# Three phases of a routed-attention block: separate loops with keys folded into queries, and one schedule of slots with queries, keys and row-tiled scores

## What is computed

```python
# x: 16 batches of 256 rows of 128
mod = (silu(c) @ wmod)                                  # shifts, scales and gates, per batch
h = layernorm(x) * (1 + ca) + sa
x = x + ga * causal_attention(h, W, b)                  # "first attention": one head, 256 x 256
h = layernorm(x) * (1 + cb) + sb
# light: windows of 128 rows, 8 heads of 64
xn = rmsnorm(h, gamma_light)
light = softmax(q @ k.T * 64**-0.5) @ v @ wo_light      # q, k, v = xn @ wq, xn @ wkv, per window and head
# selection: 50 iterations of a soft top-k on 2 scores per row, then the top 128 rows
def body(_, ab):
    a = logk - logsumexp(s + b)
    b = -relu(s + a)
scores = exp(s + a + b); sel, idx = top_k(scores, n)
# heavy: 128 selected rows attend to all 256 rows of their batch, 8 heads of 64
heavy = softmax(qh @ kh.T * 64**-0.5) @ (vh * scores_kv) @ wo_heavy
x = x + gb * (light + scatter(heavy * scores_q))
```

## Time and profile before

| | us |
|---|---|
| median of 3 runs | 541.76 (539.86 to 545.21) |
| the profiled execution | 540.5 |
| its span, first to last instruction | 538.7 |
| TensorE busy | 480.9 |
| ScalarE busy | 396.4 |
| VectorE busy | 387.7 |
| GpSimd busy | 259.9 |

### The profile page before, as it was taken

One profiled execution on the slowest core, in us unless ns is written; L12 is line 12 of the kernel. 1 busy time (PEld: TensorE's weight loads), 2 busy tenths in 40 slices (PEclk: granted clock), 3 DMA queues, 4 the chain that ended last, 5 costly groups with the idle time before them and its releaser, 6 DMA issues.

```text
span 538.7 us, 12047 instructions
## 1 busy us (share of the span) xinstructions
PE 480.9 (89%) x3805; PEld 414.2 (77%) x3805; DVE 387.7 (72%) x1311; ACT 396.4 (74%) x1480; POOL 259.9 (48%) x294
## 2 busy tenths in 40 slices
PE   2498878766999999999999798899999999999995
PEld 1386656545888888888888676798898988888984
DVE  5539999985888888888888798365656656556652
ACT  2269899856999999999999567666666676666662
POOL 6316577772334333334433123454556665556555
PEclk9999999978999999999999889999999999999998
DMA  8740101100000000000000000000000100000101
GB/s 233 258 204 2 31 21 31 31 30 19 2 12 12 12 11 11 12 11 12 11 12 12 12 10 12 21 19 8 12 12 11 16 16 12 12 12 11 16 7 16
DMA packets 18398, 16.42 MB, mean 30 GB/s; under 512 B 1984, under 2 KB 17104, under 8 KB 18080
## 3 DMA queue, kind: packets, MB, share of 16 engines
q1 hardware_dynamic: 14336, 11.83, 6.8%
q0 software_dynamic: 3248, 3.41, 3.7%
q10 hardware_dynamic: 752, 0.40, 0.3%
HBM read 10.36 MB, written 5.28 MB: 29 GB/s over the span
## 4 chain that ended last, share of the span: by engine, by line
PE 69%; DVE 7%; ACT 2%; issue 1%; POOL 1%; POOLq 0%; DVEq 0%
PE bank L651 13%; PE bank L653 10%; PE bank L652 10%; PE bank L884 6%; PE bank L932 6%; PE bank L834 6%; PE bank L916 5%; PE bank L852 5%; PE bank L819 4%; PE bank L949 2%; ACT pr L584 1%; DVE left L1250 1%; DVE top_at L1251 1%; DVE nmx L1218 1%; DVE top_all L1247 1%
## 5 line engine op out<-in xcount | busy, mean ns | idle before, releaser
L402 POOL TENSOR_TENSOR pr<-pr,rinv 128x512 f32<-128x512 f32 x64 | 66.7, 1042 | 134.8 <-DVE rinv L1224 134.7
L417 POOL TENSOR_TENSOR pr<-pr,rinv 128x512 f32<-128x512 f32 x64 | 72.5, 1133 | 76.6 <-DVE rinv L1327 76.4
L584 ACT ACTIVATE pr<-bank,nmx 128x128 f32<-128x128 f32 x256 | 89.7, 364 | 8.0 <-DVE nmx L1218 7.9
L628 ACT ACTIVATE pr<-bank,nmx 128x256 f32<-128x256 f32 x128 | 59.7, 472 | 34.0 <-DVE nmx L1321 33.9
L1218 DVE TENSOR_REDUCE nmx<-bank 128x4 f32<-128x512 f32 x64 | 43.5, 680 | 28.8 <-PE bank L653 27.2
L584 ACT ACTIVATION_READ_ACCUMULATOR pr<-bank,nmx 128x1 f32 x256 | 52.5, 205 | 0.0
L819 PE MATMUL bank<-ident,pr 128*128 128x128 f32 x256 | 39.6, 278 | 5.8 <-POOL pr L402 5.8
L1321 DVE TENSOR_REDUCE nmx<-bank 128x2 f32<-128x512 f32 x64 | 43.8, 684 | 0.7 <-PE bank L653 0.4
L884 PE MATMUL bank<-xq,T_w 128*128 128x128 f32 x256 | 41.8, 286 | 0.4 <-ACT xq L613 0.4
L638 ACT ACTIVATE pt<-bank 128x512 f32<-128x512 f32 x64 | 38.4, 600 | 1.4 <-PE bank L916 1.4
L916 PE MATMUL bank<-ident,pr 128*128 128x128 f32 x256 | 38.5, 273 | 0.4 <-POOL pr L417 0.4
(11 more groups left out here) (231 smaller groups left out, 1506.9 us busy)
## 6 DMA issues: line engine op xcount, KB each, us to landing
mod_bc<-mod_rows_scratch SPq DMA_DIRECT2D x1, 3072.0 KB, 11.1
X<-in_L_attn_x SPq DMA_DIRECT2D x4, 512.0 KB, 10.3
xh_scratch<-xhs SPq DMA_DIRECT2D x16, 128.0 KB, 1.8
out<-X SPq DMA_DIRECT2D x16, 128.0 KB, 1.8
mod_bc<-mod_rows_scratch SPq DMA_DIRECT2D x1, 1024.0 KB, 4.2
wkv_raw<-in_L_ffn_wkv_light SPq DMA_DIRECT2D x1, 512.0 KB, 11.8
wmod_sb<-in_L_wmod ACTq DMA_DIRECT2D x1, 384.0 KB, 5.1
wq_raw<-in_L_ffn_wq_heavy POOLq DMA_DIRECT2D x1, 256.0 KB, 7.5
```

Of the source, the lines that this page charges most:

```text
L402: pool.tensor_tensor(q, q, rinv[k % 4][:, :, None].broadcast_to([P, 4, P]), ALU.mult)\
L417: pool.tensor_tensor(q, q, rinv[k % 4][:, 0:2, None].broadcast_to([P, 2, N]), ALU.mult)\
L584: act.activation(pr[k % 4][:, i * P:(i + 1) * P], ps[2 + k % 2][:, i * P:(i + 1) * P], ACT.Exp, bias=nmx[k % 4][:, i:i + 1], accum_out=sum ...
```

## The change

The three pipelines become one list of (phase, lag, function) for each engine, run in 158 slots. Batch b of first attention starts in slot 5b/2 rounded down, light unit g in slot 14 + g, heavy unit g in slot 78 + g; selection's steps have slots of their own between 49 and 76. `early` now holds only what the weights' preparation needs, and PSUM banks are given to uses by tables (`FILL_BANKS` before slot 14, `A_BANKS` after); P^T has one bank instead of two, light values and output share one.

Scores come from queries and keys: `Q_w`, `K_w` (split raw weights) instead of the product `U_w`; `QH_w` (f32), `KH_w` instead of `T_w`. The scores are f32 matmuls with 64 contraction rows, even heads in rows 0 to 63 and bank 2, odd heads in rows 64 to 127 and bank 3. Q and K are one f32 copy each, on ScalarE or VectorE in turn, and no low half.

An iteration of selection works on e = exp(s - c): u becomes the sum over min(e, u)/k, one VectorE instruction; the base c is renewed twice (`SEGMENTS`), with one exp and one ln each. `xhat` moves from VectorE to GpSimd. The two broadcasts of gamma (`gam_bc`) go.

```diff
+A_AT = [5 * b // 2 for b in range(B)]
+SCORES_AT = A_AT[-1] + 12
+H0 = SCORES_AT + 29
+L0 = H0 - 4 * B
+END = H0 + 4 * B + 16
+
+
+def run_slots(stages):
+
+    for t in range(END):
+        for phase, lag, f in stages:
+            if phase == "A":
+                if t - lag in A_AT:
+                    f(A_AT.index(t - lag))
+            elif phase == "L":
+                if 0 <= t - lag - L0 < 4 * B:
+                    f(t - lag - L0)
+            elif phase == "H":
+                if 0 <= t - lag - H0 < 4 * B:
+                    f(t - lag - H0)
+            else:
+                f(t)
...
+        SEGMENTS = (0, 17, 33, CD_ITERS - 1)
+        ITERATIONS_AT = {SCORES_AT + at: (n, n + count) for at, n, count in (
+            (3, 0, 6), (4, 6, 6), (5, 12, 5), (8, 17, 6), (9, 23, 6), (10, 29, 4), (13, 33, 6), (14, 39, 6), (15, 45, 4))}
+        LN_AT = [SCORES_AT + at for at in (6, 11, 16)]
+        TOP_AT = SCORES_AT + 18
...
+        A_LAGS = {"s": 4, "x": 13, "h": 2, "qk": 3, "o": 7, "p": 5, "v": 4}
+        A_BANKS = {"x": 5, "h": 5, "s": 1, "o": 1, "p": 5, "qk": 1, "v": 5}
+        FILL_BANKS = {"x": 6, "h": 5, "s": 2, "o": 3, "p": 4, "qk": 1, "v": 5}
...
-                    mm = triple(ps[7 * (j == 1)][:, i * N:(i + 1) * N], [u[:, 2 * j + i, :] for u in U_w],
+                    c = 2 * (j % 2) + i
+                    mm = triple(ps[7 * (j == 1)][:, i * N:(i + 1) * N], [w[:, c * P:(c + 1) * P] for w in (Q_w, K_w)[j // 2]],
                                 (XT_hi[:, b, :], XT_lo[:, b, :]))
-                mm.then_inc(lt["up"], 1)
-
...
-            def scores(p, k):
...
-                at_least(pe, lt["p"], 4 * (g - 1))
-                triple(ps[2 + k % 2][:, :].rearrange("p (h t) -> p h t", h=4),
-                       [t[:, b, w * P:(w + 1) * P] for t in (XT_hi, XT_lo)],
...
+            def scores(g):
...
+                at_least(pe, lt["p"], 8 * window)
+                for c in range(4):
+                    for i in range(2):
+                        rows = slice(i * DH, (i + 1) * DH)
+                        mm = pe.matmul(ps[2 + i][:, c * P:(c + 1) * P], QT[b % 2][rows, c, t], KT[b % 2][rows, c, t],
+                                       start=True, stop=True)
...
-            def scores_h(p, k):
...
-                for i in range(2):
-                    mm = triple(ps[2 + k % 2][:, i * N:(i + 1) * N], [u[:, 2 * j + i, 0:NQ] for u in U[par]],
-                                (XT_hi[:, b, :], XT_lo[:, b, :]))
...
+            def scores_h(g):
...
+                for m in range(2):
+                    for i in range(2):
+                        rows, c = slice(i * DH, (i + 1) * DH), 2 * n + m
+                        mm = pe.matmul(ps[2 + i][:, m * N:(m + 1) * N], QT[b % 2][rows, c, 0:NQ], KT[b % 2][rows, c, :],
+                                       start=True, stop=True)
                 mm.then_inc(hv["Sp"], 1)
...
+                for c in range(4):
+                    mm = pe.matmul(ps[0][:, c * NQ:(c + 1) * NQ], QH_w[:, c * P:(c + 1) * P], xq[b % 2][:, :],
+                                   start=True, stop=True)
...
+            def project_kh(g):
...
                 for i in range(2):
-                    mm = pe.matmul(ps[0][:, i * NQ:(i + 1) * NQ], T_w[:, 2 * j + i, :], xq[par][:, :],
-                                   start=True, stop=True)
-                mm.then_inc(hv["tp"], 1)
...
-            run_phases(([(0, h_transpose), (2, value_a), (3, values_a), (1, scores_a), (0, query_key),
-                             (2, p_transpose_a), (6, x_transpose)], extra_a),
-                       ([(3, scores), (0, project), (OUT_LAG, out_light), (5, p_transpose), (0, project_v), (6, values)],
-                        selection),
-                       ([(6, values_h), (0, row_transpose), (0, project_vh), (4, p_transpose_h),
-                         (0, project_h), (9, out_heavy), (1, scores_h)], None),
-                       "al al al al la la la", "lh lh lh lh lh lh lh")
+            run_slots([("A", 4, scores_a), ("A", 13, x_transpose), ("L", 7, p_transpose), ("A", 2, h_transpose),
+                       ("L", 0, project), ("A", 3, query_key), ("A", 7, values_a), ("L", 1, project_v),
+                       ("A", 5, p_transpose_a), ("H", 0, row_transpose), ("A", 4, value_a), ("H", 1, project_kh),
+                       ("H", 8, p_transpose_h), ("H", 0, project_q), ("H", 3, project_vh), ("H", 10, values_h),
+                       ("L", 9, values), ("H", 4, scores_h), ("T", 0, heavy_piece), ("H", 12, out_heavy),
+                       ("L", 10, out_light), ("T", 0, selection), ("L", 4, scores)])
...
+            def split(w, source, gamma, n):
+                dve.tensor_scalar(w[0][:, :], source, gamma, None, ALU.mult).then_inc(w_hi, 1)
+                dve.wait_ge(w_hi, n + 1)
+                dve.scalar_tensor_tensor(w[1][:, :], source, gamma, w[0][:, :].bitcast(F32), ALU.mult, ALU.subtract)\
+                    .then_inc(w_split, 1)
...
-            def cd_sums(n):
-                act.wait_ge(r["t"], n + 1)
-                at_least(act, r["ln"], n)
-                act.activation(cd_e[:, :], cd_t[:, :], ACT.Exp, accum_out=cd_sum[:, :]).then_inc(r["e"], 1)
-                act.wait_ge(r["e"], n + 1)
-                act.activation(cd_ln[:, :], cd_sum[:, :], ACT.Ln).then_inc(r["ln"], 1)
...
+            def cd_iteration(n):
+                if n in SEGMENTS:
+                    dve.wait_ge(r["e"], SEGMENTS.index(n) + 1)
+                    u = u_first
+                else:
+                    dve.wait_ge(r["u"], n)
+                    u = cd_u[(n - 1) % 2]
+                dve.scalar_tensor_tensor(cd_min[:, :], cd_e[:, :], u[:, :], inv_k[:, :], ALU.min, ALU.mult,
+                                         accum_out=cd_u[n % 2][:, :]).then_inc(r["u"], 1)
...
+            def cd_rebase(s):
+                dve.wait_ge(r["ln"], s + 1)
+                dve.tensor_scalar(cd_c[:, :], cd_ln[:, :], cd_c[:, :], 40.0, ALU.add, ALU.subtract).then_inc(r["c"], 1)
+                dve.wait_ge(r["c"], s + 2)
+                dve.tensor_scalar(cd_t[:, :], s_rows[:, :], cd_c[:, :], 70.0, ALU.subtract, ALU.min).then_inc(r["t"], 1)
...
+            run_slots([("L", 6, recip), ("T", 0, select_1), ("L", 5, neg_max_pair), ("A", 4, mask_max),
+                       ("A", 4, neg_max_a), ("L", 11, finish_light), ("A", 13, xt_lo), ("A", 9, neg_mean_rstd2),
+                       ("A", 8, ln2_stats), ("H", 11, o_evac_h), ("L", 7, pt_evac), ("L", 0, project_evac),
+                       ("A", 7, attn_out), ("A", 4, v_evac), ("T", 0, select_2), ("A", 12, keep_scores),
+                       ("H", 1, k_evac_h), ("H", 5, neg_max_pair_h), ("H", 6, recip_h), ("A", 8, aggregate),
+                       ("H", 13, finish_heavy), ("T", 0, select_3), ("T", 0, weights), ("A", 10, route),
+                       ("A", 10, norm_squares), ("H", 3, v_evac_h), ("A", 8, var_eps), ("T", 0, late_mean),
+                       ("A", 4, recip_a)])
...
+            run_slots([("L", 2, v_evac_l), ("A", 1, ln1), ("A", 13, xt_hi), ("L", 10, o_evac), ("H", 5, exps_odd_h),
+                       ("H", 8, pt_evac_h), ("H", 1, k_evac_h), ("T", 0, cd_act), ("A", 2, h_evac), ("L", 5, exps_odd),
+                       ("L", 7, pt_evac_act), ("L", 5, exps_even), ("H", 1, xq_evac), ("H", 5, exps_even_h),
+                       ("A", 3, qk_evac), ("L", 0, project_evac), ("A", 9, ln2), ("A", 5, pt_evac_a),
+                       ("H", 0, q_evac_h), ("A", 4, exps_a), ("A", 10, squares)])
...
+            run_slots([("A", 9, ln2_rstd), ("H", 14, scatter), ("A", 10, modulate), ("L", 6, normalise),
+                       ("T", 0, gather_first), ("A", 10, rms), ("A", 7, residual), ("L", 11, add_light),
+                       ("A", 11, xhat), ("H", 0, gather), ("H", 7, normalise_h)])
```

More of the change, by code:

```diff
@@ L199, in adaln_routed_attention @@
         nmxa = [sb(f"nmxa{i}", [P, C]) for i in two]
-        pa = [sb(f"pa{i}", [P, 3 * P]) for i in two]
         suma = [sb(f"suma{i}", [P, C]) for i in two]
@@ L218, in adaln_routed_attention @@
         s4 = [sb(f"s4{i}", [P, 4]) for i in two]
-        early.close()
-        sb = late
-        U = [[sb(f"U{i}{s}", [P, HEADS, N], F32R) for s in ("hi", "lo")] for i in two]
+        QT = [sb(f"QT{i}", [P, 4, N]) for i in two]
+        KT = [sb(f"KT{i}", [P, 4, N]) for i in two]
         V = [sb(f"V{i}", [P, C, HID]) for i in two]
-        pr = [sb(f"pr{i}", [P, 512]) for i in range(4)]
         nmx = [sb(f"nmx{i}", [P, 4]) for i in range(4)]
@@ L228, in adaln_routed_attention @@
         rinv = [sb(f"rinv{i}", [P, 4]) for i in range(4)]
+        tmp = [sb(f"tmp{i}", [P, D]) for i in two]
+        early = ExitStack()
+        late = sb
+        sb = lambda name, shape, dt=F32: early.enter_context(nc.sbuf_tensor(name, shape, dt))
+        wmod_sb = sb("wmod_sb", [P, 6 * D])
+        wq_raw = sb("wq_raw", [P, 2, HID])
+        wkv_raw = sb("wkv_raw", [P, 2 * HID])
+        wk_hT = sb("wk_hT", [P, 4, D])
```

(67 more changed lines are left out.)

1134 lines of the change are left out of this document (518 added, 616 removed).

## The result

| | before | after |
|---|---|---|
| median of the runs | 542.73 us (539.86 to 545.21) | 516.28 us (513.88 to 519.6) |
| ratio to before | | 0.952, 95% interval 0.944 to 0.960 |
| span of the profiled run | 538.7 us | 517.8 us |
| TensorE busy | 480.9 us, 89% | 461.0 us, 89% |

The account below looks back on a forecast made before the run. TensorE bounds most of the kernel (89% of span), ScalarE and VectorE first attention, VectorE selection's end. Start 47 + work 434 - 16 already done + tail 8 = 473; selection 8 and waits 12 give 493, plus 3: 496 us, range 472 to 528.

Parts of the forecast that it names:

- The likeliest case: Whole kernel: the sum of terms holds, 496 us, own range 478 to 510, chance 0.50.
- two rivals: ScalarE paces the overlapped slots, 518 us, chance 0.19; weight loads of the two halves don't overlap, 520, chance 0.14.
- Light scores: Light phase: 16 f32 instructions on alternating row halves take 1.03 us a window, bounds 1.78 and 2.32; batch 12.2 us.
- the rival of the other side: Light and heavy scores: halves of rows don't run together at all; 545 or 580 us, chance 0.12.
- Loads in turn: Scores: weight loads of the two halves don't overlap, light scores at 1.78 us; +24 us, 520, chance 0.14.
- Start: Before light work: VectorE begins slot 4 at about 25, ten slots of 1.90 us, slot 14 at 47 (44 to 50).
- Overlapped slots: First attention beside light work: TensorE leads at 4.61 us a slot, plus 0.3 of waits, 12 us over 36 slots.
- Selection: Selection's 9 + 8 slots: VectorE needs 3.9 to 4.7 us against TensorE's 3.05; 14 us at most, 8 taken.
- Heavy batch: Heavy phase on TensorE: 11.1 us a batch instead of 11.52, bounds 12.6 and 13.7; sixteen take 177 us.
- Light work's rest, heavy phase and end: From slot 76 on: the sum leaves 205.7 us, with heavy batches of 11.1 us and a tail of 8.
- No overlap in effect: First attention and light phase: light values first come at 138.81 as before, only the phases' gains remain; 521 us, chance 0.05.
- the marks given: Signs of being right: TensorE at least 93% of span, first QT projection before 55 us, light scores 1.0 to 1.1 us.

Follow-up runs that it names:

- the fastest kernel: Kernel after, with the selection iterations' exponentials in PSUM and light output in bank 5 from the 13th window on: 502.5 us, 0.929 of before.

## Why the prediction was right, and where it was not

Faster by over 1%, forecast at 0.88, and 516 lies in 472 to 528. The likeliest case said 496, 20 us too low, outside its own range of 478 to 510. It is the width of the range that holds the result: two rivals had 518 and 520, nearest to it, and neither of their mechanisms came about. By the terms of its sum, on the profiled span (517.8 against 493):

**Light scores: right.** 1.03 forecast, 1.09 measured; light batch 12.2 forecast, 12.33 measured where nothing disturbs it (the kernel without overlap, from 271 us on). The mechanism named for it, halves running together, is shown by the run without it: 566.0 us, between the 545 and 580 given to the rival of the other side. "Loads in turn" has fallen: the light block takes 1.09, not 1.78, with alternating halves., the one 64-row row of before, was no bad price for halves that don't alternate: 0.145 us an instruction, 0.124 in that run.

**Start: 4 us short, most of it scatter.** Slot 14 at 51.05 against 47; it came at 48.3 when the kernel ran again, and at 47.7 to 49.5 in the variants with the same code up to there. The sum let ten slots run at VectorE's 1.90 us.

**Overlapped slots: right.** From its own terms, first attention's remaining 46 us, 36 units of light work (110), 11 of waits, less what the lags leave over at slot 50 (some 14: three transposes, four values blocks, five outputs at rates of the earlier trace rows and two scores; this is an estimate made afterwards), 153 us; measured 51.05 to 203.18, 152.1. TensorE stands still for 8.6 us of it, where 11 were given. ScalarE did not pace them: it is busy 131.7 us of the 152.1, TensorE 143.5.

**Selection: the term that failed, 8 us forecast, 21 measured (19 when run again).** The load of VectorE was right in kind. The sum over it was not: "14 us at most" is what its slots of 3.9 us give (17 x 0.85). With its other price, 9 slots of 4.7 and 8 of 3.9, it is 9 x 1.65 + 8 x 0.85 = 22, so the forecast's own upper bound holds what was measured, and 8 was taken under a bound set too low. And two things were not in it. The iteration was priced by a top round, which reads one tensor; with two in SBUF it collides with GpSimd, on average 0.595 us and 0.07 for the sum instead of at most 0.55. And "banks are shared in turn: fits" looked at P^T alone: with values and output in one bank, VectorE's lateness stops TensorE at once. With both mended the excess is 6.5 us, near the 8 forecast. Nor was there a term for TensorE's clock, 0.95 in these slots: some 5 us of the 21.

**Heavy batch: 11.1 forecast, 11.38 measured, 16 x 0.28 = 4.5 us.** Scores 1.06 for 1.03 twice, K 1.64 for 1.60 and Q 0.99 for 0.89 make 0.20 of it. The earlier trace rows had priced only projections behind f32; Q behind transposes is dearer too. The other 0.08 is open.

**Light work's rest, heavy phase and end (slot 76 on): 8 us short in all**, 214.1 measured where the sum leaves 205.7, the 4.5 among them. Two more are the drain: TensorE waits twice 0.78 us for P^T in its one bank, and once 0.50 for GpSimd. Some 2 us are not accounted for.

```profile
502.84 0.63 PE L923 MATMUL bank<-ident,pr 128*128 128x128 f32 x4 [0.78 <-ACT pt L649]
503.39 1.09 PE L939 MATMUL bank<-pt,V 128*64 128x128 f32 x16
...
506.43 0.63 PE L923 MATMUL bank<-ident,pr 128*128 128x128 f32 x4 [0.78 <-ACT pt L649]
```

**No overlap in effect: mis-sized.** 521 was given; the run shows 565. The rival took first attention at its old 4.76 us a batch, which the new slots don't keep without light work in them (7.06). What the new scores bring inside the new schedule, against the old ones, was not run.

Of the marks given, TensorE at 93% of the span did not come (89%, and 91% in the fastest kernel); it is the same miss, the selection's.

## What to carry over

When a new instruction is priced by its nearest row, compare where the operands lie as well as how many elements they have: with two SBUF operands an iteration took 1.13 to 1.30 us when it started under a multiplication of GpSimd, and 0.44 to 0.56 otherwise. Multiply a bound out at both prices before calling it the most. List for each PSUM bank who must empty it, and ask what happens when that engine is late; a free bank was worth as much here as the faster iteration. A schedule of slots is tuned by its collisions: changing the spacing from 2.5 to 2.25 slots (with the places of the iterations), or one place in a slot's order, cost 22 and 12 us in kernels whose work was the same.

## What the runs showed of the hardware that was not expected

Two halves of rows overlap on TensorE even when four instructions of one half come before four of the other: 1.07 us for 8 of 256 columns, as when they alternate (1.06), against 1.92 without a second half. With eight and eight of 128 columns only part overlaps (1.64, against 1.09 and 1.98). A 64-row f32 instruction alone is not cheaper than one of 128 rows (1.92 us for eight, and 1.54 or 1.72).

The Trainium skill ("TensorEngine Tiling (Array Packing)", Key Properties) says that different tiles can load weights and multiply in parallel. The runs agree for halves of rows: 1.06 us for the heavy block against 1.92 when all of it is in one half. For halves of columns no run took the neighbour away.
